# Two graph layers: the second layer's weights turned partly by TensorE and partly by DMA

## The reference, cut to what matters

```python
h = x @ W
e = leaky_relu((h @ a_src)[:, None] + (h @ a_dst)[None, :], 0.2)
valid = (adj > 0) & (h.sum(axis=1) != 0)[None, :]
att = where(valid, softmax(where(valid, e, -1e9), axis=1), 0.0)
attention = where(att >= 1e-4, att, 0.0) * valid.sum(axis=1)[:, None]   # 0 if the row's top is not over 1e-4
x = layernorm(x + elu(h + attention @ h))

scores = leaky_relu(x @ ks.T, 0.2)
attn = softmax(where(adj > 0, scores, -9e15), axis=1)
x = layernorm(x + attn @ ks)
```

## Time and profile before

| | |
|---|---|
| time, median of 3 runs (lowest, highest) | 854.62 us (854.02, 854.94) |
| span of the profiled execution | 855.3 us |
| instructions | 17732 |
| mean granted clock of PE | 0.991 of full |
| PE busy | 827.0 us, 97% |
| DVE busy | 788.1 us, 92% |
| ACT busy | 760.6 us, 89% |
| POOL busy | 224.9 us, 26% |
| chain that ended last | PE 83%, DVE 9%, ACT 4% |

### The profile page before, as it was taken

The page is one execution under the profiler, slowest core; times in us unless marked ns, Lnnn a source line. Parts: engine busy times, 40 slices in busy tenths (PEclk is TensorE's granted clock), DMA queues, the critical chain, the costliest instruction groups (busy, mean ns, idle before and its releaser), DMA issues.

```text
span 855.3 us, 17732 instructions
## 1 busy us (share of the span) xinstructions
PE 827.0 (97%) x7139; PEld 714.2 (84%) x7139; DVE 788.1 (92%) x1009; ACT 760.6 (89%) x732; POOL 224.9 (26%) x446
## 2 busy tenths in 40 slices
PE   7489999999999999999999999999999999999997
PEld 7468888888998888889888888988888898888876
DVE  3999999999999999999999999999999999997865
ACT  2899999999999999999999999999999999998763
POOL 2033232323312233332223333222233321222100
PEclk9799999999999999999999999999999999999999
DMA  9999786666688766668866667886666678611000
GB/s 212 239 131 172 151 149 102 122 130 131 141 155 148 106 120 130 132 139 154 151 104 122 130 131 139 153 153 104 126 124 136 135 151 155 103 31 24 13 2 10
DMA packets 39969, 106.07 MB, mean 124 GB/s; under 512 B 11088, under 2 KB 23504, under 8 KB 32208
## 3 DMA queue, kind: packets, MB, share of 16 engines
q0 software_dynamic: 20864, 66.06, 53.5%
q1 hardware_dynamic: 18592, 38.80, 12.7%
q10 hardware_dynamic: 432, 0.07, 0.1%
HBM read 138.48 MB, written 2.10 MB: 164 GB/s over the span
## 4 chain that ended last, share of the span: by engine, by line
PE 83%; DVE 9%; ACT 4%; issue 2%; DMA 1%; POOLq 0%; POOL 0%; ACTq 0%; DVEq 0%
PE work L290 23%; PE sums L410 23%; PE sums L438 12%; PE work L381 6%; PE work L382 6%; PE work L386 6%; PE sums L439 6%; DVE att1T L996 2%; DVE att L908 2%; ACT att L677 1%; ACT att L634 1%; PE sums L444 1%; PE work L315 1%; ACT att L654 1%; ACT att0T L666 1%
## 5 line engine op out<-in xcount | busy, mean ns | idle before, releaser
L290 PE MATMUL work<-ident,att 128*128 128x128 f32 x2072 | 256.2, 275 | 14.0 <-DVE att L1098 12.6
L290 PEld LDWEIGHTS work<-ident,att 128*128 128x128 f32 x2072 | 233.6, 142 | 22.7 <-DVE att L1098 13.0
L410 PE MATMUL sums<-h_all,att0T 128*128 128x128 f32 x2048 | 244.2, 275 | 0.0
L410 PEld LDWEIGHTS sums<-h_all,att0T 128*128 128x128 f32 x2048 | 236.1, 192 | 0.1
L438 PE MATMUL sums<-k_parts,att1T 128*128 128x257 f16 x1024 | 182.3, 274 | 0.3 <-DVE att1T L996 0.2
L439 PE MATMUL sums<-k_parts,att1T 128*128 128x129 f16 x1024 | 177.3, 218 | 0.0
L996 DVE SCALAR_TENSOR_TENSOR att1T<-work,att1T 128x1024 f16<-128x1024 f32 x128 | 152.3, 1209 | 12.9 <-ACT att1T L687 12.8
L687 ACT ACTIVATE att1T<-work 128x1024 f16<-128x1024 f32 x127 | 129.4, 1029 | 27.9 <-PE work L290 27.9
L921 DVE SCALAR_TENSOR_TENSOR att<-att,cut 128x2048 f32<-128x2048 f32 x62 | 145.2, 2346 | 0.0
L672 ACT ACTIVATE att<-work 128x1024 f32<-128x1024 f32 x128 | 127.7, 1028 | 19.5 <-PE work L386 19.5
L960 DVE CUSTOM_DVE_ANT_0 att<-att,mask 128x2048 f32<-128x2048 f32 x62 | 141.3, 2282 | 2.0 <-ACT att L672 2.0
(11 more groups left out here) (123 smaller groups left out, 669.6 us busy)
## 6 DMA issues: line engine op xcount, KB each, us to landing
mask<-adj POOLq DMA_DIRECT2D x31, 1024.0 KB, 8.6
mask_zero<-zero_cols SPq DMA_DIRECT2D x29, 1024.0 KB, 5.0
mask_zero<-adj POOLq DMA_DIRECT2D x29, 1024.0 KB, 11.7
att<-x SPq DMA_DIRECT2D x4, 512.0 KB, 6.7
k_parts<-ks POOLq DMA_DIRECT2D x2, 1024.0 KB, 19.7
x_sb<-x SPq DMA_DIRECT2D x32, 64.0 KB, 2.8
out<-x SPq DMA_DIRECT2D x32, 64.0 KB, 4.8
mask<-adj POOLq DMA_DIRECT2D x2, 512.0 KB, 6.6
```

The costliest lines, as they stand in the source:

```text
L290: mm = pe.transpose(place[:, b * P:(b + 1) * P], source(c * PER + b), ident[:, :])
L410: mm = pe.matmul(acc0, att0T[:, k * P:(k + 1) * P], h_all[:, k, :], start=(k == 0), stop=(k == BLOCKS - 1))
```

## The change

- Layer 1's weights are turned in two ways. The first 12 blocks (`WHOLE_BLOCKS`, columns 0 to 1535) are turned by PE in two fills of six, copied in f32 and multiplied in f32 with an f32 copy of k (`k_whole`). The last 20 blocks (2560 columns) are split in SBUF before they are turned: ACT writes the high part (`split_high`), DVE the low part in two pieces of 1280 columns into the end of `att1` itself (`low_part1`), and SP turns them by DMA (`turn_high`, `turn_low`). PE sums them a slot later (`sum_split`), with three products for each block (129, 128 and 129 columns), all into one `acc1` of 129 columns; `finish1` so has one step less.
- The next tile's `bend1` now waits, beside its scores, until the DMA has read the low parts out of `att1` (chunks 2 and 3).
- The zeros' copies and the adding load are gone; `zero_mask` is a minimum of two bf16 tiles for every tile, into the one `mask_zero`; there are four mask buffers.
- `raise0` is one pass over 4096. `raise1` has parts of 1536 and 2560 columns. PSUM places rotate in the order in which PE fills them (`FILLS`).
- `x1` has three buffers; several small tiles are written in place. The last tile's 20 blocks are turned by PE (`last_high1`, `last_low1`, `last_sum`).
- All engines have new written orders: first slots 0 to 4, `slot(t)` for 5 to 26, last slots.

SP, the turning by DMA and the slot's order:

```diff
+            def turn_high(u):
+                sp.wait_ge(high_ready, u + 1)
+                if u > 0:
+                    sp.wait_ge(summed1, 4 * u)
...
+                sp.dma_start_transpose(high1T.rearrange("p (b r) -> p b r", r=P), high1[:, :]).then_inc(high_turned, 16)
+            def turn_low(u, i):
+                sp.wait_ge(low1, 2 * u + (1 if i == 1 else 2))
+                if u > 0:
+                    sp.wait_ge(summed1, 4 * u)
...
+                sp.dma_start_transpose(low1T[:, piece(i)].rearrange("p (b r) -> p b r", r=P),
+                                       att1_halves[:, low_at(i)]).then_inc(low_turned[i], 16)
...
             def slot(t):
...
+                store(t - 4)
+                turn_high(t - 1)
+                turn_low(t - 1, 1)
+                turn_low(t - 1, 0)
+                load_x(t + 1)
```

PE, the sums of layer 1 and the slot's order:

```diff
+            def sum_whole(u, i):
+                pe.wait_ge(copied1, 2 * u + i + 1)
+                if i == 0:
+                    if u > 0:
+                        pe.wait_ge(res1_ready, u)
...
+                for k in fill_blocks(i):
+                    mm = pe.matmul(acc1, whole1T[:, k * P:(k + 1) * P], k_whole[:, k, :], start=(k == 0), stop=False)
+                mm.then_inc(summed1, 1)
+
+            def split_sum(blocks):
+                for b in blocks:
...
+                    pe.matmul(acc1, high1T[:, part], k_parts[:, k, 0:D + 1], start=False, stop=False)
+                    pe.matmul(acc1[:, 0:D], high1T[:, part], k_parts[:, k, D + 2:], start=False, stop=False)
+                    mm = pe.matmul(acc1, low1T[:, part], k_parts[:, k, 0:D + 1], start=False, stop=(b == BLOCKS - 1))
                 mm.then_inc(summed1, 1)
...
             def slot(t):
-                u, w = t - 1, t - 2
-                score(u, 3)
+                score(t - 1, 3)
                 turn0(t, 0)
                 turn0(t, 1)
                 turn0(t, 2)
+                turn0(t, 3)
                 sum0(t, 0)
-                turn0(t, 3)
                 sum0(t, 1)
                 sum0(t, 2)
-                turn1(u, 0, True)
                 sum0(t, 3)
-                turn1(u, 1, True)
-                if w >= 0:
-                    sum1(w, 2)
-                    sum1(w, 3)
-                turn1(u, 2, True)
-                turn1(u, 3, True)
-                sum1(u, 0)
+                turn1(t - 1, 0)
+                sum_split(t - 2, 0)
+                sum_split(t - 2, 1)
+                turn1(t - 1, 1)
+                sum_whole(t - 1, 0)
                 turn_q(t)
-                sum1(u, 1)
-                for c in range(3):
-                    score(t, c)
+                sum_whole(t - 1, 1)
+                score(t, 0)
+                score(t, 1)
+                score(t, 2)
```

ACT (the slot's order now: `q_high_part(t)`, `bend0(t + 2)`, `bend1(t, 0)` to `(t, 3)`, `copy0(t + 1, 0)` to `(t + 1, 3)`, `raise0(t + 2)`, `raise1(t, 0)`, `raise1(t, 1)`, `elu_exp(t + 1)`, `copy1(t, 0)`, `split_high(t)`, `copy1(t, 1)`):

```diff
             def bend1(u, c):
                 act.wait_ge(scored, 4 * u + c + 1)
                 if u > 0:
...
+                    for i in range(2):
+                        if low_at(i).start < 2 * (c + 1) * CHUNK and low_at(i).stop > 2 * c * CHUNK:
+                            act.wait_ge(low_turned[i], 16 * u)
...
+            def split_high(u):
+                act.wait_ge(exp1, 2 * u + 2)
+                if u > 0:
+                    act.wait_ge(high_turned, 16 * u)
+                nc.scalar.activation(high1[:, :], att1[:, WHOLE_COLS:N], ACT.Copy, scale=LIFT).then_inc(high_ready, 1)
```

DVE (the slot's order now: `mask0(t + 2)`, `residual0(t)`, `threshold0(t + 1)`, `cut(t + 1, 0)`, `elu(t)`, `finish1(t - 2)`, `normalise0(t)`, `low_part1(t - 1, 1)`, `q_low_part(t)`, `low_part1(t - 1, 0)`, `cut(t + 1, 1)`, `build_mask(t + 3)`, `normalise1(t - 3)`, `zero_mask(t + 3)`, `mask1(t, 0)`, `mask1(t, 1)`, `offset1(t)`):

```diff
             def zero_mask(f):
...
+                nc.vector.tensor_tensor(mask_zero[:, :], mask[f % MASKS][:, :], zero_cols[:, :],
+                                        ALU.min).then_inc(zero_masked, 1)
...
+            def low_part1(u, i):
+                dve.wait_ge(high_ready, u + 1)
+                if i == 0:
+                    dve.wait_ge(low1, 2 * u + 1)
+                nc.vector.scalar_tensor_tensor(att1_halves[:, low_at(i)], att1[:, piece_cols(i)], LIFT, high1[:, piece(i)],
                                                ALU.mult, ALU.subtract).then_inc(low1, 1)
```

More of the change, by code:

```diff
@@ L282, in _ @@
+            first_slots()
+            for t in range(5, TILES - 5):
                 slot(t)
+            last_slots()
             for p in range(2):
@@ new lines, in first_slots @@
+                bend1(2, 1)
+                bend1(2, 2)
+                bend1(2, 3)
+                copy0(3, 0)
+                copy0(3, 1)
+                copy0(3, 2)
+                copy0(3, 3)
+                raise0(4)
+                raise1(2, 0)
+                raise1(2, 1)
+                elu_exp(3)
+                split_high(2)
+                copy1(2, 0)
+                q_high_part(3)
+                copy1(2, 1)
+                bend0(5)
+                bend1(3, 0)
+                bend1(3, 1)
@@ new lines, in first_slots @@
+                mask1(2, 1)
+                zero_mask(5)
+                offset1(2)
+                mask0(5)
+                residual0(3)
+                threshold0(4)
+                elu(3)
+                finish1(1)
+                normalise0(3)
+                low_part1(2, 1)
+                q_low_part(3)
+                low_part1(2, 0)
+                cut(4, 0)
+                cut(4, 1)
+                build_mask(6)
+                normalise1(0)
+                mask1(3, 0)
+                mask1(3, 1)
@@ new lines, in first_slots @@
+                zero_mask(6)
+                offset1(3)
+                mask0(6)
+                residual0(4)
+                threshold0(5)
+                elu(4)
+                finish1(2)
+                normalise0(4)
+                low_part1(3, 1)
+                q_low_part(4)
+                low_part1(3, 0)
+                normalise1(1)
+                cut(5, 0)
+                cut(5, 1)
+                build_mask(7)
+                mask1(4, 0)
+                mask1(4, 1)
+                zero_mask(7)
@@ L1239, in last_slots @@
                 last = TILES - 1
+                mask0(last - 2)
+                residual0(last - 4)
+                normalise1(last - 7)
+                threshold0(last - 3)
+                elu(last - 4)
+                finish1(last - 6)
+                normalise0(last - 4)
+                low_part1(last - 5, 1)
+                q_low_part(last - 4)
+                low_part1(last - 5, 0)
+                cut(last - 3, 0)
+                cut(last - 3, 1)
+                mask1(last - 4, 0)
@@ new lines, in last_slots @@
+                build_mask(last - 1)
+                mask1(last - 4, 1)
+                zero_mask(last - 1)
+                offset1(last - 4)
+                mask0(last - 1)
+                residual0(last - 3)
+                threshold0(last - 2)
+                elu(last - 3)
+                finish1(last - 5)
+                normalise0(last - 3)
+                low_part1(last - 4, 1)
+                q_low_part(last - 3)
+                low_part1(last - 4, 0)
+                cut(last - 2, 0)
@@ L1412 @@
+            first_slots()
+            for t in range(5, TILES - 5):
+                slot(t)
+            last_slots()
 def kernel(x, adj, L0_gnn_W, L0_gnn_a, L1_gnn_ks):
```

979 lines of the change are left out of this document (583 added, 396 removed).

## The result

The changed kernel takes 830.67 us (median of 4, 830.16 to 831.39) against 854.32 before: ratio 0.9719, interval 0.9703 to 0.9735, 2.8% faster. The forecast was 816 us, the range 806 to 880; of the 38.6 us that were forecast, 23.7 came. The sign came out as forecast, and so did the lists of PE and DVE. The forecast's own case (810 to 826 us) did not come: the time lies where rival 3 has it (826 to 850), by the second cause that is named there, a D between 8.4 and 9.4 us.

A forecast was written before the change was run, and what follows sets the result against it. PE's list bounds the kernel: the slot falls from 24.87 to 23.6 us (PE 23.39 plus 0.2 stall), transfers cost nothing. 855.3 - 31 x (24.87 - 23.6) + 0.4 = 816.3, stated as 816 us, range 806 to 880.

The forecast's parts named there:

- the lists of PE and DVE: Work per slot: PE 23.39 us, 1.46 less than before; DVE 23.11 us busy, about 23.4 needed with gaps.
- The forecast's own case: Slot of 23.4 to 23.9 us, time 810 to 826 us; chance 0.58.
- rival 3: DVE sets the slot through waits, or D of 8.4 to 9.4 us does; 826 to 850 us, chance 0.14.
- D: Time from the end of `split_high` to the last low piece's landing; put at 7.1 us, limit 8.4.
- signs of being wrong: Turns landing after over 5 us, ACT idling at `bend1(t, 2)` or `(t, 3)`, or DVE never idle with slot over 24.
- The stall behind `finish1`: PE waits ahead of `sum_whole` until `finish1` has read `acc1`; some 0.1 to 0.2 us per slot, taken as 0.2.
- The transfers: Turning on SP's queue at the copy's rate or somewhat less, costed at nothing; 228 KB per us needed for that.
- 15.2 + D: Least slot: ACT's 15.2 us from the start of `bend1(t+1, 3)` to the end of `split_high(t+1)`, plus D.
- Rival 1: DMA too slow: `bend1(t+1, 3)` waits for the last low piece, D from 9.7 us; 912 us at a third of copy's rate; chance 0.19.
- Rival 2: Blocks turned by DMA one after another, each with its own latency; some 4,000 us, or 2,200 by the skill's figure; chance 0.03.
- the ends: Before the first `turn_q` +1.3 us; behind the last one +1.1 and -2; net +0.4 us.
- the base: The profiled execution's span was taken as 0.7 us above the median of the runs, so 816.3 became 815.6 us.

The follow-up runs named there:

- experiment 5: `finish1` about 0.2 us shorter (the addition doesn't wait for its own reciprocal, tile 2 to 29), in the kernel of experiment 1: 821.31 us, ratio 0.9597.
- experiment 6: Changed kernel with 14 blocks turned by PE and 18 by DMA instead of 12 and 20: 835.27 us, ratio 0.9759.
- Experiment 8: 10 blocks turned by PE and 22 by DMA, in the kernel of experiment 1: 828.59 us, ratio 0.9684.
- experiment 1: Changed kernel with SP issuing the two low pieces ahead of the high part: 824.42 us, ratio 0.9638.
- experiment 2: Changed kernel with low pieces turned from the high part's buffer, so that `bend1` waits for no transfer: 823.56 us, ratio 0.9626.
- experiment 3: Changed kernel with `raise1`'s second part cut into four passes, making ACT's list some 0.5 us longer per slot: 844.80 us, ratio 0.9873.
- experiment 4: Kernel of experiment 1 with `raise1`'s second part cut into four passes, making ACT's list some 0.5 us longer per slot: 828.75 us, ratio 0.9683.
- experiment 7: Changed kernel with 10 blocks turned by PE and 22 by DMA instead of 12 and 20: 850.04 us, ratio 0.9932.

## Why the prediction was right, and where it was off

The time lies in the stated range, but that is in part the width of the range. Two of the prediction's own signs of being wrong came: ACT idles at `bend1` of the third and fourth chunk (17 waits, 9.4 us), and the high part lands after 5.1 us, over the 5 that were named (the low pieces take 3.6). The mean slot, 23.97 us, is above the forecast's 23.4 to 23.9. What came is the second half of rival 3, to which, with its first half, the prediction gave 0.14.

**PE's list: right.** Forecast 23.39 us plus 0.2 of stall; measured 23.41 plus 0.28. A split block takes 3.41 / 20 = 0.171 us, where the old pair with the same columns and one weight load less took 0.168. The stall behind `finish1` was named with its place, and experiment 5 shows it. That it grows when DVE is late from its own list was named too; experiment 6 shows that.

**DVE and ACT: right.** `low_part1` 1.49 against 1.46, `zero_mask` 2.29 against 2.28, DVE's need 23.37 against 23.4. Experiment 8 shows that DVE sets the slot when PE has 0.33 less. ACT waits some 0.9 us per regular slot for `turn_q`, against 1.1 forecast.

**The transfers: the term that was mis-sized.** The prediction took "the copy's rate or somewhat less, and cost it at nothing". The turning runs at 213 KB per us, half the copy's rate. D was put at 7.1 us, as 3.7 until DVE has made the last piece plus 3.4 until that has landed, with a limit of 8.4. Measured, it is 3.7 + 0.8 + 3.7 = 8.2 in a regular slot. The 0.8 us are SP's: it is still issuing the other pieces, a cost that the prediction put at nothing without a row for it. The pauses raise D to 8.5 to 9.15 in single slots, its mean is 8.5, and the 0.16 us from a landing to the start of `bend1` had no term either. The form of the bound, 15.2 + D against PE's slot, was right: experiments 1 to 4 and 7 move the time by its first side, in both directions, and experiment 6 by PE's. Rival 1 (D from 9.7 on) wasn't the outcome, but the wait that it describes is what took the missing us.

The Trainium skill (DMA: Bandwidth & Descriptors, Latency and other measured facts) has 261 GB/s for a transpose whose middle dimension isn't contiguous. The trace gives less, 213 KB per us or about 218 GB/s, as the slope between the two sizes. Rival 2 is out: 20 blocks land in 5.1 us, and in a row one costs 0.15 us. The 1309 ns that the Trainium skill (VectorE: DVE Perf Modes, The three transpose paths) gives for one 128 x 128 block by DMA isn't tested by any run here.

**The account.** The span forecast was 816.3, the span found 828.4, 12.1 us more:

- 31 x 0.09 = 2.8 us: the regular slot is 23.69, not 23.6 (the stall behind `finish1`, 0.08).
- 31 x (23.97 - 23.69) = 8.7 us: the long slots. Some 4.1 are in the 20 middle slots (0.20 each) and are D's, as experiments 1 and 2 show, and so are the 0.9 of the slot before them (24.57 here, 23.68 in both experiments). 2.5 are the one slot of 26.2; the rest is in the other slots at both ends and wasn't looked into.
- 0.5 us: the ends. The first `turn_q` came at 56.7 (58.1 forecast) and the last part took 28.6 us (26.8 forecast); two misses that mostly cancel, which is luck.

The rest is the base. The two spans differ by 26.9 us and the medians by 23.7. The profiled execution of the changed kernel took 830.16 us with a span of 828.4, so 1.8 us lie around it. As much lies around the spans of the kernel before in the experiments' runs, so its profiled execution took some 857.1, 2.5 above its median; the prediction, which set the span directly against the median, allowed 0.7 for it. In those runs that kernel took either 854.0 to 855.3 or 856.6 to 857.2 us, and the profiled execution was one of the longer ones.

## What to carry to other kernels

A wait that closes a loop over two engines has its own sum: here 15.3 us of ACT's work, the time to the landing, and the 0.16 us until ACT starts. An engine's idle time elsewhere in the slot is no reserve for it, and with a reserve of 0.1 us the order of the issues on one queue was worth 6 us. Of transfers issued together, the one for which an engine waits soonest goes first, not the one that is ready first. And where a term of the sum has no row, it pays to write down the rate at which it starts to cost: here that limit (223 KB per us) was close above what was measured (213), and it showed which term to look at.

## What the runs showed of the hardware that was not expected

**The issue of a DMA transpose holds its queue.** SP is busy 2.67, 3.03 and 3.33 us (18, 20 and 22 blocks; the shortest of the landings 4.6, 5.0 and 5.2): 0.15 us per block of 32 KB, the same as the slope of the landings. The rate of the turning may be that of its issue; this is read from rows, not tested.

**A pause in the turning.** In the slots from the seventh to the twentieth `turn_q`, five issues took 0.6 to 0.95 us longer than the rest (the two low pieces counted as one row), and in each of them the DMA engines moved one 16 KB packet of the instruction queue; none of the others has one. The DMA view of such a window, 444.5 to 448.5 us in 40 slices:

```profile
GB/s 223 220 207 228 220 207 228 215 195 172 177 162 126 215 233 192 172 287 164 113 36 0 0 0 0 0 3 8 8 10 10 10 10 8 31 284 292 297 289 287
...
q8 instruction: 1, 0.02, 1.4%
```

The turning stops for 1.3 us and goes on. This is what makes a slot with 0.1 us of reserve long: D is 9.15 us in this one. That the instruction load causes the pause is inferred from the coincidence alone; nothing was run that moves the loads.

**GpSimd steps of 0.3 us take up to 6.8.** POOL is busy for 478 us, where it was 225. The small product `coef` took 0.30 us in every middle slot of the kernel before. Now it takes 4.5 to 6.8 there (4.6 in the mean over all slots):

```profile
473.18 6.76 POOL L1644 TENSOR_SCALAR coef<-gate,rz 128x1 f32<-128x1 f32 x1
```

It starts while DVE makes `zero_mask` from two tensors in SBUF (473.14) and ends at 479.94, just when DVE's two `mask1` passes, which also read two tensors in SBUF, have ended (479.86, the rows above). Before, `coef` fell beside DVE's low parts, which read one input from PSUM, and wasn't held. The Trainium skill (SBUF — State Buffer, SBUF: two separate sides) says that a DVE instruction with two SBUF inputs and a GpSimd one that reads SBUF exclude each other for the whole instruction, and the trace agrees. In the middle slots no other engine waited for it. In the last ones DVE waited four times, 0.7 to 1.0 us, for a square root on POOL; whether the same cause is behind these isn't shown.
